# First layer's scores of a fused two-layer kernel: four fp32 products on 16 rows each, or two float32r products on 128 stacked rows

## The chip, the cores and the metric

One core of one Trainium2 chip runs the whole kernel. The metric is the device time of one execution in microseconds. The engines are TensorE (PE, with its weight loads PEld), VectorE (DVE), ScalarE (ACT), GpSimd (POOL) and SyncE (SP), which issues most of the DMAs.

## The reference

Two transformer-like layers over `x` of 16 x 256 x 256. What matters here is the attention of the first layer, with 16 heads of 16 values each:

```
q, k = rope(q), rope(k)                       # 16 heads, Dh = 16
scores = einsum('bhtd,bhsd->bhts', q, k) / sqrt(Dh)
scores = where(causal, scores, -inf)
probs = softmax(scores); out = einsum('bhts,bhsd->bhtd', probs, v)
return out @ w_out.T + b_out
```

Ahead of it stands a small cross attention with `fside`, behind it a category-dependent product and a gated feed-forward with blockwise fp4 rounding of activations and weights. The second layer (another attention, a routed feed-forward) follows. All inputs are float32.

## The kernel before

The program is written engine by engine; each engine runs its list in order, and semaphores tie the lists together. The first layer is a software pipeline over batches b from -2 to 17 (`B` is 16) with eight slots p each. A slot is one pair of heads: P = 8b + p. In a slot each engine does its part of the pair's attention, and beside it one piece of other work of the batch behind or ahead. All matmuls except those of heads and of some small products are written as three float32r products of a rounded part (`hi`) and a rest (`lo`): `matmuls3`.

The path of queries and keys, for batch b+1 during batch b:

- PE `project` (slots 1 and 2: queries, keys) writes even and odd components to bank 5; DVE `add_qk` adds the bias into `qk0`.
- POOL `rotate` (slot 3 in the steady state, both sides) multiplies with cosine and sine (two operations of 512 columns) and adds or subtracts (two of 256) into `QK0`. In the first batch DVE does the keys' part in `rotate_first`.
- SP `rotated` writes `QK0` to `d_rot` in device memory and reads it back with four DMAs into `Rs[b % 2]`, so that the 16 components of each head lie on 16 partitions that begin at a multiple of 32.

In slot p PE runs `scores(P + 1)`: for the two heads g, and for the two halves `st` of the queries, one fp32 product with 16 contracted rows, 128 queries and 128 or 256 keys (lines 338 to 342). Each appears as two instructions in the profile, eight in all. Then DVE `maxima` masks and takes the row maxima into `Ph`, ACT `exps` takes exponentials and sums, PE `turn_heads` transposes, ACT `copy_turned` copies to `PTh`, and PE `values` takes the product with the values every second slot.

The other work in a round of eight slots that the prediction names: slot 0 `turn_sums` (waits for both `multiply` of DVE into `hb`), `first_values`, `spread_sums`; slot 1 `project(b+1, 0)`, `turn_hidden`, on DVE `normal_out`, `hidden_steps` (L885, L888, L890) and `hidden_low`, on ACT `hidden_high` (`hqT_hi`); slot 2 `project(b+1, 1)`, `project_out`, DVE `add_attention`; slot 3 `turn_hidden`, `category`; slots 4 and 5 `down` and `project_v`, then `first_scores` and `turn_category`; slots 6 and 7 `gate` and `up`, with ACT `tanh` and DVE `gated`. POOL `rounded` does the rounding steps of the feed-forward (L1079, L1081, L1094), in slots 0, 2 and 4. During the first four batches the weights are rounded and split as well, in slots listed in `MEASURE`, `ROUND` and `TURN`. SP's list for a batch is `load_in(b+2)`, `load_category(b)`, `rotated(b+1)`. In the last rounds the generators of the second layer are started (`run(following, ...)`), and SP loads that layer's projection weights into `raw1`.

## Time and profile before

| what | value |
|---|---|
| median of 3 runs | 2471.0 us (2461.97, 2471.0, 2471.63) |
| span of the profiled execution | 2475.1 us |
| PE busy | 2335.6 us, 94% |
| DVE, ACT, POOL busy | 1840.2, 1276.7, 1039.9 us |
| first scores, last scores of the first layer | 49.6 us, 757.0 us |

The page gives the span of the profiled execution, from its first to its last instruction, and no separate time for it; it stands 4.1 us above the median of the three runs. Matmuls overlap in the records, so that the distance from one start to the next tells more than the duration of one. A line number with PE can be that of a helper: L55 is every product made with `matmuls`, L136 every transpose, L340 only the scores of the first layer.

### The profile page before, as it was taken

The page shows a single profiled execution, that of the slowest core. Times are in us where ns is not written, and L with a number is a line of the kernel's source. Part 1 is how long each engine was busy: PE and PEld are TensorE (multiplying, and loading weights), DVE is VectorE, ACT ScalarE, POOL GpSimd, SP SyncE. Part 2 cuts the span into 40 slices and gives each one's busy share as a digit, 9 for nine tenths or more (in the row PEclk, how much of TensorE's full clock was granted, in tenths as well). Part 3 has the DMA queues.
Part 4 walks back from the last instruction along what each step waited for, and adds up shares of the span by engine and source line. Part 5 has one row for each costly group of instructions (what it writes and reads, how often), then busy time and mean ns, then how long its engine had stood idle before and what let it go on. Part 6 is the DMA issues. An engine that isn't in the chain of part 4 may idle for free.

```text
span 2475.1 us, 55054 instructions
## 1 busy us (share of the span) xinstructions
PE 2335.6 (94%) x19136; PEld 2091.7 (85%) x19136; DVE 1840.2 (74%) x5136; ACT 1276.7 (52%) x3807; POOL 1039.9 (42%) x1090
## 2 busy tenths in 40 slices
PE   4899999999997799999999999889999999999999
PEld 3677887878876678888888887789999999999999
DVE  5777777777777766666666665568878888888876
ACT  2666566665654355555555555424325555555522
POOL 4545545446453545545545545123332222222063
PEclk7899999999998999999999999999999999999999
DMA  4321211211220221221122122132116777777444
GB/s 114 107 52 46 56 38 51 54 46 47 47 86 10 63 55 44 50 56 46 47 56 50 47 52 69 43 69 43 39 30 234 236 233 240 232 228 240 149 118 126
DMA packets 153080, 225.73 MB, mean 91 GB/s; under 512 B 54294, under 2 KB 123174, under 8 KB 142054
## 3 DMA queue, kind: packets, MB, share of 16 engines
q1 hardware_dynamic: 143942, 203.56, 28.6%
q0 software_dynamic: 8864, 18.66, 2.9%
q8 instruction: 154, 2.52, 0.5%
q14 instruction: 120, 0.98, 0.2%
HBM read 159.32 MB, written 27.16 MB: 75 GB/s over the span
## 4 chain that ended last, share of the span: by engine, by line
PE 69%; DVE 13%; POOL 7%; issue 5%; ACT 5%; DMA 1%; POOLq 0%; SPq 0%; DVEq 0%; ACTq 0%
PE bank L55 54%; PE bank L136 7%; PE bank L340 2%; POOL P L1743 2%; PE bank L367 2%; PE bank L1253 2%; PE bank L1293 1%; ACT Ph L622 1%; DVE xe L885 1%; ACT PTh L634 1%; POOL Qn L1768 1%; POOL Qn L1766 1%; DVE tb L1606 1%; POOL xr_lo L1775 1%; DVE Ph L771 1%
## 5 line engine op out<-in xcount | busy, mean ns | idle before, releaser
L1447 ACT ACTIVATE P<-P,mx 128x144 f32<-128x144 f32 x512 | 206.2, 405 | 264.1 <-DVE mx L1568 263.2
L2579 POOL DMA_INDIRECT xE<-d_y,ixs x78 | 112.5, 1442 | 336.0 <-PE bank L136 305.8
L55 PE MATMUL bank<-xD_hi,w1e_lo 128*128 128x256 f32 x880 | 251.1, 285 | 0.0
L55 PE MATMUL bank<-w2e_hi,hrD_hi 128*128 128x256 f32 x880 | 249.0, 283 | 0.0
L55 PE MATMUL bank<-w2e_lo,hrD_hi 128*128 128x256 f32 x880 | 248.9, 283 | 0.0
L55 PE MATMUL bank<-w2e_hi,hrD_lo 128*128 128x256 f32 x880 | 248.9, 283 | 0.0
L1743 POOL TENSOR_TENSOR P<-P,rs 128x512 f32<-128x512 f32 x128 | 133.3, 1042 | 273.8 <-DVE rs L1577 270.3
L1079 POOL TENSOR_TENSOR xe<-xe 128x704 f32<-128x704 f32 (+3 forms) x64 | 88.4, 1381 | 376.0 <-DVE xe L890 375.8
L55 PE MATMUL bank<-xD_lo,w1e_hi 128*128 128x256 f32 x880 | 245.9, 279 | 0.0
L55 PE MATMUL bank<-xD_hi,w1e_hi 128*128 128x256 f32 x880 | 245.6, 279 | 0.0
L2188 ACT ACTIVATE hD<-bank,b1E 128x256 f32<-128x256 f32 x312 | 127.0, 473 | 197.2 <-PE bank L55 182.8
L2281 DVE TENSOR_TENSOR hrD_lo<-hD,hrD_hi 128x512 fp32r<-128x512 f32 x284 | 197.3, 695 | 9.7
L622 ACT ACTIVATE Ph<-Ph,mx 128x128 f32<-128x128 f32 x256 | 101.0, 394 | 188.5 <-DVE mx L771 188.5
L2279 DVE CAST hrD_hi<-hD 128x512 fp32r<-128x512 f32 x284 | 121.4, 428 | 101.3 <-ACT hD L2188 100.7
L1568 DVE CUSTOM_DVE_ANT_0 P<-bank,maskb 128x144 f32<-128x144 f32 x512 | 126.1, 302 | 77.5 <-PE bank L1253 77.5
L771 DVE CUSTOM_DVE_ANT_0 Ph<-bank,maskb 128x128 f32<-128x128 f32 (+1 forms) x512 | 151.5, 350 | 28.1 <-PE bank L340 28.0
L55 PE MATMUL bank<-xr_hi,w_lo 128*128 128x256 f32 x512 | 157.7, 308 | 13.7 <-DVE fa L1640 11.0
L55 PEld LDWEIGHTS bank<-w2e_hi,hrD_lo 128*128 128x128 f32 x880 | 168.7, 192 | 0.0
L55 PEld LDWEIGHTS bank<-w2e_hi,hrD_hi 128*128 128x128 f32 x880 | 168.7, 192 | 0.0
L55 PEld LDWEIGHTS bank<-w2e_lo,hrD_hi 128*128 128x128 f32 x880 | 168.7, 192 | 0.0
L55 PEld LDWEIGHTS bank<-xD_hi,w1e_lo 128*128 128x128 f32 x880 | 165.6, 188 | 0.0
L55 PEld LDWEIGHTS bank<-xD_lo,w1e_hi 128*128 128x128 f32 x880 | 165.4, 188 | 0.0
(324 smaller groups left out, 8005.1 us busy)
## 6 DMA issues: line engine op xcount, KB each, us to landing
w1raw<-in_ew SPq DMA_DIRECT2D x39, 1024.0 KB, 5.7
w2raw<-in_ew SPq DMA_DIRECT2D x39, 1024.0 KB, 4.9
K<-Kn SPq DMA_DIRECT2D x256, 72.0 KB, 2.1
Q<-Qn SPq DMA_DIRECT2D x256, 64.0 KB, 2.0
d_ys<-oE SPq DMA_DIRECT2D x39, 256.0 KB, 2.7
d_rot<-QK SPq DMA_DIRECT2D x16, 512.0 KB, 2.9
Rs<-d_rot SPq DMA_DIRECT2D x64, 128.0 KB, 4.4
b2E<-in_eb SPq DMA_DIRECT2D x39, 128.0 KB, 3.6
```

What stands on the lines that cost most here:

```text
L55: inst = e.matmul(out, l, r, start=k == 0, stop=k == len(pairs) - 1)
L136: inst = e.transpose(o, i, ident[0:i.shape[0], 0:i.shape[0]])
L622: e.activation(dst[:, 0, :], dst[:, 0, :], ACT.Exp, bias=mx[:, 0, n:n + 1], scale=-1.0, accum_out=rs[:, 0, n:n + 1])
L771: inst = e.tensor_tensor_reduce(dst[:, st:2 * st + 1, :], bank[:, 128 * st:128 + 256 * st].rearrange("p (a n) -> p a n", n=128), mask(128 ...
L1079: e.tensor_tensor(x, x, s, ALU.add).then_inc(*po.up())
L1447: inst = e.activation(P1[t % 2][:, n, :], P1[t % 2][:, n, :], ACT.Exp, bias=mx1[t % 2][:, 2 * g + sg:2 * g + sg + 1], scale=-1.0, accum_ou ...
L1568: inst = e.tensor_tensor_reduce(P1[t % 2][:, 2 * sg + g, :], banks[6 + g][:, 144 * sg:144 * sg + 144], mask(144), -1.0, 1e30, ALU.add, ALU ...
L1743: e.tensor_tensor(P[:, :, 16:144], P[:, :, 16:144], r.broadcast_to((128, 4, 128)), ALU.mult).then_inc(*po.up())
L2188: inst = e.activation(hD[:, 2 * (n % 2) + m, :], halves(n)[:, m, :], ACT.Gelu if q < 0 else ACT.Gelu_apprx_tanh, bias=bias[:, f:f + 1])
L2279: e.tensor_copy(hr[0], h).then_inc(*vs.up())
L2281: e.tensor_tensor(hr[1], h, hr[0].bitcast(F32), ALU.subtract).then_inc(v_h, 1)
L2579: e.indirect_dma_start(out=xE[q % 2][c], out_offset=None, in_=d_y, in_offset=bass.IndirectOffsetOnAxis(ap=ixs[r % 4][:, c:c + 1].bitcast(U ...
```

## The change

- `QK0` becomes two tensors: `QKl` takes the rotated values, ACT (`heads_high`) writes their float32r rounding to `QKh`, POOL (`heads_low`) replaces `QKl` by the rest.
- DVE `add_qk` becomes `turn_qk`: bias addition and product with cosine and sine in one operation per component (512 columns each), into `rt0`. POOL's `rotate` keeps only the subtraction and the addition and moves to slots 1 and 2; `rotate_first` goes.
- SP writes for each side of q and k three copies to `d_rot`: for queries rounded, rounded, rest; for keys rest, rounded, rounded. `load_heads(L)` reads, for the two slots of pair L, 48 rows per head into partitions 0 to 47 and 64 to 111 of `QS`, which is cleared once at the start. The keys of the two heads have separate column blocks. There are two such buffers; they are used in turn.
- A slot's scores are two products on 128 rows: queries 128 to 255 with 2 x 256 keys into bank 0, queries 0 to 127 with 2 x 128 keys into bank 1. The maxima read them from there.
- SP's order: the loads for pair 4b+2, then `load_in`, the loads for 4b+3, `write_heads` for queries, `load_category`, `write_heads` for keys, the loads for 4b+4 and 4b+5. The second layer's weights are loaded after those for pair 63. In the stages behind it two semaphores are used again with an offset, with no change of order.

```diff
-        QK0, q0 = tile("QK0", 4, 256), tile("q0", 2, 256)
+        QKh, q0 = tile("QKh", 4, 256, dt=F32R), tile("q0", 2, 256)
...
-        rt0, qk0 = folded(rots[:, 0, :], (2, 2, 256)), folded(rots[:, 1, :], (2, 2, 256))
+        rt0 = [folded(rots[:, i, :], (2, 2, 256)) for i in range(2)]
...
+        QKl = tile("QKl", 4, 256, dt=F32R)
+        stack0 = tile("stack0", 12 * 256, dt=F32R)
+        QS = stack0.rearrange("p (h j x n) -> p h j x n", h=2, j=2, x=3)
...
-            def rotated(b, between=None):
-
-                e.wait_ge(g_rot, 2 * b + 2)
-                e.dma_start(d_rot[b].rearrange("q e p n -> p (q e) n"), QK0).then_inc(l_rw, 16)
-                if between is not None:
-                    load_block(between)
-                e.wait_ge(l_rw, 16 * (b + 1))
-                if b >= 2:
-                    e.wait_ge(p_S, 8 * (b - 1))
-                rows = d_rot[b].rearrange("q e (r j h) n -> j (e r) q (h n)", j=4, h=4)
-                for j in range(4):
-                    e.dma_start(Rs[b % 2][32 * j:32 * j + 16].rearrange("r q h n -> r q (h n)"), rows[j]
-                                ).then_inc(l_R[b % 2], 16)
+            def write_heads(b, qk):
+                if not 0 <= b < B:
+                    return
+                high, low = ((0, 1), 2) if qk == 0 else ((1, 2), 0)
+                src = [x[:, 2 * qk:2 * qk + 2, :].bitcast(F32) for x in (QKh, QKl)]
+                e.wait_ge(c_qh, 2 * b + qk + 1)
+                for s in high:
+                    e.dma_start(d_rot[b, qk, s].rearrange("e p n -> p e n"), src[0]).then_inc(l_rw, 16)
+                e.wait_ge(g_rot, 2 * b + qk + 1)
+                e.dma_start(d_rot[b, qk, low].rearrange("e p n -> p e n"), src[1]).then_inc(l_rw, 16)
+            def load_heads(L):
+                if not 0 <= L < 4 * B:
+                    return
+                b, h = divmod(L, 4)
+                if h == 0:
+                    e.wait_ge(l_rw, 96 * (b + 1))
+                if L >= 2:
+                    e.wait_ge(p_S, 2 * L - 2)
+                else:
+                    e.wait_ge(g_V, 4)
+                rows = d_rot[b].rearrange("x s e (r j g h) n -> g h (s e r) j x n", j=2, g=2, h=4)
+                for g in range(2):
+                    for x in range(2):
+                        e.dma_start(QS[64 * g:64 * g + 48, L % 2, :, x * (g + 1), :].bitcast(F32), rows[g, h][:, :, x, :]
+                                    ).then_inc(l_R[L % 2], 16)
 
...
-            rotated(0, 7)
+            write_heads(0, 0)
+            write_heads(0, 1)
+            load_block(7)
+            load_heads(0)
+            load_heads(1)
             load_block(8)
             load_category(0)
             for n in range(9, 12):
                 load_block(n)
+            load_heads(2)
             load_in(2)
-            for n in range(12, 15):
+            for n in range(12, 14):
                 load_block(n)
-            rotated(1)
+            load_heads(3)
+            load_block(14)
+            write_heads(1, 0)
+            write_heads(1, 1)
+            load_heads(4)
+            load_heads(5)
             load_block(15)
             load_x(2)
             for b in range(1, B):
+                if b == B - 1:
+                    run(following, 1)
+                load_heads(4 * b + 2)
                 if b + 2 < B:
                     load_in(b + 2)
+                load_heads(4 * b + 3)
+                write_heads(b + 1, 0)
                 if b == B - 1:
                     run(following, 1)
                 load_category(b)
-                if b + 1 < B:
-                    rotated(b + 1)
+                write_heads(b + 1, 1)
+                load_heads(4 * b + 4)
+                load_heads(4 * b + 5)
 
 
...
-                b, p = divmod(P, 8)
                 bank = banks[0:2]
                 if P:
                     e.wait_ge(v_mx, 2 * P)
-                if p == 0:
-                    e.wait_ge(l_R[b % 2], 64 * (b // 2 + 1))
-                j = [32 * (2 * (P % 2) + g) for g in range(2)]
-                q, k = ([Rs[b % 2][j[g]:j[g] + 16, x, p // 2, :] for g in range(2)] for x in range(2))
-                for st in range(2):
-                    for g in range(2):
-                        inst = e.matmul(bank[g][:, 128 * st:128 + 256 * st], q[g][:, 128 * st:128 * st + 128],
-                                        k[g][:, 0:128 * st + 128], start=True, stop=True)
-                inst.then_inc(p_S, 1)
+                L = P // 2
+                if P % 2 == 0:
+                    e.wait_ge(l_R[L % 2], 64 * (L // 2 + 1))
+                q, k = QS[:, L % 2, P % 2, 0, :], QS[:, L % 2, P % 2, 1:3, :]
+                e.matmul(bank[0][:, :], q[:, 128:256], k, start=True, stop=True)
+                e.matmul(bank[1][:, 0:256].rearrange("p (g n) -> p g n", g=2), q[:, 0:128], k[:, :, 0:128],
+                         start=True, stop=True).then_inc(p_S, 1)
 
...
+            def heads_high(b, qk):
+                if not 0 <= b < B:
+                    return
+                part = slice(2 * qk, 2 * qk + 2)
+                e.wait_ge(g_t, 2 * b + qk + 1)
+                e.activation(QKh[:, part, :], QKl[:, part, :].bitcast(F32), ACT.Copy).then_inc(c_qh, 1)
...
+                    if p == 1:
+                        heads_high(b + 1, 0)
+                    if p == 3:
+                        heads_high(b + 1, 1)
...
                         inst = e.tensor_tensor_reduce(
-                            dst[:, st:2 * st + 1, :], bank[:, 128 * st:128 + 256 * st].rearrange("p (a n) -> p a n", n=128),
+                            dst[:, st:2 * st + 1, :],
+                            banks[1 - st][:, 128 * (st + 1) * g:128 * (st + 1) * (g + 1)].rearrange("p (a n) -> p a n", n=128),
...
-            def add_qk(b, qk):
+            def turn_qk(b, qk):
                 if not 0 <= b < B:
                     return
                 e.wait_ge(p_qk, 2 * b + qk + 1)
                 if b:
-                    e.wait_ge(g_rot, max(2, 2 * b + qk - 1))
+                    e.wait_ge(g_t, 2 * b + qk - 1)
                 for eo in range(2):
-                    inst = e.tensor_scalar(qk0[:, qk, eo, :], halves(5)[:, eo, :], b_qk0[:, 2 * qk + eo:2 * qk + eo + 1],
-                                           None, ALU.add)
+                    inst = e.scalar_tensor_tensor(
+                        out=rt0[qk][:, eo], in0=halves(5)[:, eo:eo + 1, :].broadcast_to((128, 2, 256)),
+                        scalar=b_qk0[:, 2 * qk + eo:2 * qk + eo + 1], in1=rot0[:, eo:eo + 2, :], op0=ALU.add, op1=ALU.mult)
                 inst.then_inc(v_rq, 1)
-
-            def rotate_first():
-
-                rt = [OT0, Wc]
-                e.wait_ge(v_rq, 2)
-                for eo in range(2):
-                    e.tensor_tensor(rt[eo], qk0[:, 1, eo:eo + 1, :].broadcast_to((128, 2, 256)), rot0[:, eo:eo + 2, :],
-                                    ALU.mult).then_inc(*vs.up())
-                e.wait_ge(s_v, vs.n)
-                e.tensor_tensor(QK0[:, 2, :], rt[0][:, 0, :], rt[1][:, 0, :], ALU.subtract)
-                e.tensor_tensor(QK0[:, 3, :], rt[0][:, 1, :], rt[1][:, 1, :], ALU.add).then_inc(g_rot, 1)
 
...
             def rotate(b, qk):
                 if not 0 <= b < B:
                     return
                 e.wait_ge(v_rq, 2 * b + qk + 1)
-                for eo in range(2):
-                    e.tensor_tensor(rt0[:, eo], qk0[:, qk, eo:eo + 1, :].broadcast_to((128, 2, 256)), rot0[:, eo:eo + 2, :],
-                                    ALU.mult).then_inc(*po.up())
                 if b >= 1:
-                    e.wait_ge(l_rw, 16 * b)
-                e.wait_ge(s_p, po.n)
-                e.tensor_tensor(QK0[:, 2 * qk, :], rt0[:, 0, 0, :], rt0[:, 1, 0, :], ALU.subtract).then_inc(*po.up())
-                e.wait_ge(s_p, po.n)
-                e.tensor_tensor(QK0[:, 2 * qk + 1, :], rt0[:, 0, 1, :], rt0[:, 1, 1, :], ALU.add).then_inc(g_rot, 1)
-                e.wait_ge(g_rot, max(2, 2 * b + qk + 1))
+                    e.wait_ge(l_rw, 96 * b)
+                t = QKl[:, 2 * qk:2 * qk + 2, :].bitcast(F32)
+                e.tensor_tensor(t[:, 0, :], rt0[qk][:, 0, 0, :], rt0[qk][:, 1, 0, :], ALU.subtract)
+                e.tensor_tensor(t[:, 1, :], rt0[qk][:, 0, 1, :], rt0[qk][:, 1, 1, :], ALU.add).then_inc(g_t, 1)
+                e.wait_ge(g_t, 2 * b + qk + 1)
+            def heads_low(b, qk):
+                if not 0 <= b < B:
+                    return
+                part = slice(2 * qk, 2 * qk + 2)
+                e.wait_ge(c_qh, 2 * b + qk + 1)
+                e.tensor_tensor(QKl[:, part, :], QKl[:, part, :].bitcast(F32), QKh[:, part, :].bitcast(F32), ALU.subtract
+                                ).then_inc(g_rot, 1)
+                e.wait_ge(g_rot, 2 * b + qk + 1)
 
...
+            e.memset(stack0.bitcast(F32), 0.0).then_inc(g_V, 1)
+            e.wait_ge(g_V, 4)
...
-                    if b == 0 and p == 2:
-                        rotate(1, 1)
-                    if p == 3 and b != 0:
+                    if p == 1:
                         rotate(b + 1, 0)
+                    if p == 2:
+                        rotate(b + 1, 1)
+                        heads_low(b + 1, 0)
                     if p == 3 and b >= -1:
                         first_query(b + 2)
-                    if p == 3 and b >= 1:
-                        rotate(b + 1, 1)
+                    if p == 3:
+                        heads_low(b + 1, 1)
```

## Rows read from the trace of the kernel before

**Rows 1.** The page: span of the profiled execution.

```profile
span 2475.1 us, 55054 instructions
```

**Rows 2.** Busy time by stretch, 300 to 400 us, PE, PEld, DVE, ACT, POOL; PEclk, DMA share, GB/s.

```profile
300.00:400.00 100.00, 97.91 (x799) 80.80 (x798) 76.35 (x249) 60.11 (x217) 52.26 (x43) 1.00 0.22 53
```

**Rows 3.** Chain that ended last, 300 to 350 us: start us, us, what.

```profile
302.58 0.85 PE bank L340 x8
...
310.24 2.11 PE bank L55 x12
...
326.86 0.85 PE bank L340 x8
...
327.71 1.63 PE bank L55 x12
...
347.37 0.85 PE bank L340 x8
```

**Rows 4.** PE timeline, 404 to 450 us: start, us, instructions, [idle before <-releaser].

```profile
404.44 0.92 PE L340 MATMUL bank<-Rs 16*128 16x128 f32 x8
...
412.48 0.38 PE L136 MATMUL bank<-ident,rs 128*16 128x128 f32 x2 [0.21 <-DVE hb L919]
...
416.38 0.92 PE L340 MATMUL bank<-Rs 16*128 16x128 f32 x8
...
421.78 0.86 PE L367 MATMUL bank<-PTh,Vp 128*32 128x256 f32 x16 [0.69 <-ACT PTh L634]
...
426.58 0.92 PE L340 MATMUL bank<-Rs 16*128 16x128 f32 x8
...
428.15 0.82 PE L136 MATMUL bank<-ident,hq 128*128 128x128 f32 x6
...
431.70 0.86 PE L367 MATMUL bank<-PTh,Vp 128*32 128x256 f32 x16
...
442.90 0.92 PE L340 MATMUL bank<-Rs 16*128 16x128 f32 x8
...
444.54 0.43 PE L55 MATMUL bank<-wgT_hi,xqT_lo 128*128 128x352 f32 x1
```

**Rows 5.** ACT timeline of the same round.

```profile
414.63 0.60 ACT L660 ACTIVATE x_hi<-bank 128x512 fp32r<-128x512 f32 x1 [1.36 <-PE bank L55]
...
420.06 0.60 ACT L704 ACTIVATE hqT_hi<-bank 128x512 fp32r<-128x512 f32 x1
...
423.94 0.40 ACT L622 ACTIVATE Ph<-Ph,mx 128x128 f32<-128x128 f32 x1 [2.21 <-DVE mx L771]
```

**Rows 6.** DVE timeline of the same round.

```profile
405.41 0.29 DVE L771 CUSTOM_DVE_ANT_0 Ph<-bank,maskb 128x128 f32<-128x128 f32 x1 [0.27 <-PE bank L340]
...
418.97 0.88 DVE L829 TENSOR_SCALAR rot0s<-bank,b_qk 128x256 f32<-128x256 f32 x2 [0.41 <-PE bank L55]
...
420.36 0.88 DVE L885 SCALAR_TENSOR_TENSOR xe<-hb,qr 128x704 f32<-128x704 f32 x1
...
426.69 0.88 DVE L795 SCALAR_TENSOR_TENSOR X<-bank,b_out,X 128x256 f32<-128x256 f32 x2 [1.45 <-PE bank L55]
...
434.90 1.34 DVE L885 SCALAR_TENSOR_TENSOR xe<-c,qr 128x512 f32<-128x512 f32 x1
...
443.64 0.69 DVE L903 TENSOR_TENSOR xqT_lo<-bank,xqT_hi 128x512 fp32r<-128x512 f32 x1 [0.37 <-ACT xqT_hi L684]
```

**Rows 7.** POOL timeline: a startup row, then the same round.

```profile
2.25 1.96 POOL L1101 MEMSET Vp<- 128x1024 f32 x2
...
422.51 1.71 POOL L1079 TENSOR_TENSOR xe<-xe 128x704 f32<-128x704 f32 x1 [5.98 <-DVE xe L890]
...
427.51 2.50 POOL L1063 TENSOR_TENSOR rot0s<-rot0s,rot 128x512 f32<-128x512 f32 x2
```

**Rows 8.** Issues of the scores' operand loads: duration ns min/median/max, first and last start; landing.

```profile
L285 SPq DMA_DIRECT2D Rs<-d_rot x64: 319/423/916, 39.4 to 710.0; - x64
...
DMA to landing us min/median/max: 3.2/4.4/5.5
```

More of the change, by code:

```diff
@@ L169, in program @@
         P0 = tile("P0", 2, 256)
-        Rs = [tile(f"Rs{i}", 2, 4, 256) for i in range(2)]
+        QKl = tile("QKl", 4, 256, dt=F32R)
+        stack0 = tile("stack0", 12 * 256, dt=F32R)
+        QS = stack0.rearrange("p (h j x n) -> p h j x n", h=2, j=2, x=3)
         Vp = [tile(f"Vp{i}", 4, 8, 32) for i in range(2)]
@@ L766, in maxima @@
                     n = 2 * p + g
-                    bank, dst = banks[g], Ph[P % 2][g]
+                    dst = Ph[P % 2][g]
                     if P >= 2:
@@ L1008, in dve_ab @@
                     if p == 1:
-                        add_qk(b + 1, 0)
+                        turn_qk(b + 1, 0)
                         normal_out(b - 1)
@@ L1129, in pool_ab @@
                         rounded(n, *blocks[n][0].shape)
-                    if b == 0 and p == 1:
-                        rotate(1, 0)
                     if b >= B - 1:
@@ L1203, in sync_c @@
                 e.dma_start(zs[:, i, :], a[src].broadcast_to((128, B))).then_inc(l_c, 16)
+            yield
             for c in range(6):
@@ L1860, in program @@
             ("ew1", 2), ("ew2", 2), ("er", 2), ("ex", 2), ("eb", 2), ("o", 2), ("ix", 4), ("cg", 8)))
-        l_out = sem("l_out")
+        l_out, LOUT = l_in, 48 * B
         p_up, p_trD, p_trE, p_down, p_ty, p_rt, p_rank = (sem(f"p_{n}") for n in ("up", "trD", "trE", "down", "ty", "rt", "rank"))
-        c_g, c_f2, c_yr, c_w2E, c_gate = (sem(f"c_{n}") for n in ("g", "f2", "yr", "w2E", "gate"))
+        c_g, c_f2, c_w2E, c_gate = (sem(f"c_{n}") for n in ("g", "f2", "w2E", "gate"))
+        c_yr, CY = c_qh, 2 * B
         v_h, v_x, v_f2, v_R, v_yD, v_lg, v_mm, v_rk, v_slot, v_tab, v_cb, v_w2E = (sem(f"v_{n}") for n in (
@@ L2044, in sync_e @@
                 e.dma_start(out[j * 128:j * 128 + 128, :], R[:, j, :]).then_inc(l_out, 16)
-            e.wait_ge(l_out, 16 * 32)
+            e.wait_ge(l_out, LOUT + 16 * 32)
         def picked_up(e, i, n):
@@ L2133, in turn_y @@
                 if b:
-                    e.wait_ge(c_yr, b)
+                    e.wait_ge(c_yr, CY + b)
                 turn(e, [(halves(7)[:, st, k * 128:k * 128 + 128], y[:, k, st * 128:st * 128 + 128])
```

9 lines of the change are left out of this document (4 added, 5 removed).

## The prediction

> **What bounds the kernel now.** I took the stretches first. The change touches the first layer, and in its steady part PE is busy 97.91 of 100 us at granted clock 1.00, with DVE at 76, ACT at 60, POOL at 52 and the DMA engines at a share of 0.22 [rows 2]. That looks like a TensorE bound. The chain of waits comes second. It passes the scores (L340) four times between 302.58 and 347.37, each time for 0.85 us [rows 3]. These two starts are also one round apart: 44.8 us for one batch of eight slots, with eight scores slots. So half of the scores are on this chain; the others lie beside ACT and DVE work. The timelines come third. PE waits twice in a round: 0.21 us for DVE's `hb` before the sums are turned (412.48) and 0.69 us for ACT's `PTh` before the values (421.78) [rows 4]. These waits are short, but they are the places where a faster PE only waits longer. The question is therefore how many of the eight slots can shorten the round.
>
> **Price of a slot.** Before, a slot is eight instructions in 0.85 us [rows 3]. Afterwards it is two float32r matmuls, of 512 and of 256 moving columns. Twelve float32r matmuls of 256 columns take 1.63 us, twelve of 352 take 2.11 us [rows 3]. With some 0.2 us for entering the group that is 0.12 and 0.16 us each, near 0.4 ns a column. 512 columns come to 0.22 us (my extrapolation; the trace has no such matmul), 256 to 0.12, entering costs 0.1: 0.44 us. Against 0.85 a slot saves 0.41; where both neighbours are float32r already (slot 5, between the projection of v and the second half of `down`) another 0.15 goes, since two changes of type are gone: 0.6. If nothing but the two matmuls counted, a slot would save 0.5; if the wide one cost twice what I take, 0.2.
>
> **Where the saving can be used, over one round** [rows 4].
> - 404.44 to 412.48. Behind the scores go the maxima, four exponentials, tanh, the gate product and DVE's two `hb` products; PE stands waiting for these already. DVE waits only 0.27 us for these scores before its maxima at 405.41; until then it is in its products [rows 6]. So the maxima can begin at most 0.27 us earlier. The second slot of this stretch, beside that chain, gives nothing. Gain 0.27.
> - 412.48 to 421.78. ACT runs without a gap from `x_hi` at 414.63 to 419.95, then `hqT_hi` at 420.06 and `PTh` to 421.7 [rows 5]. Only the 0.11 us before 420.06 depend on PE. Two slots lie here; gain 0.11.
> - 426.58 to 431.70. DVE adds the attention (426.69 to 427.57) [rows 6] before it takes the maxima, so the scores at 426.58 are ready in time now; then exponentials, `hqT_hi` and `PTh` until the values at 431.70. Two slots, gain 0.
> - 431.70 to 442.9 is PE's own work. One slot, gain 0.6.
> - 442.90 to 444.54. A slot and the values stand before the gate, which needs `xqT_lo`, written by DVE from 443.64 for 0.69 us less its overlap (to about 444.3) [rows 6]. Of 0.41 us, 0.2 can be used. The rest of the round has no scores.
> Sum 1.2 us of a round of 44.8.
>
> **What is added.**
> - DVE: the two bias additions of 2x256 elements (0.88 us) become two fused products of 2x512. One such op lies between 0.44 (its 256 columns now) and 0.88 us (704 columns, L885); nearest is 0.69 for 512 columns from PSUM (L903) [rows 6]. Two make 1.35: +0.5 in slot 1 and +0.5 in slot 2. In slot 2 DVE has 1.45 us idle before `add_attention` (426.69). From the projection's end (418.97) both additions are in the way, 1.0 of the 1.45; the same DVE work can start about 0.35 earlier, because slot 1's scores are shorter. Room left: about 0.8 us.
> - POOL loses the two 2x512 products per side (2.50 us for two) and gains one difference of 512 columns per side; at half of that row, 1.25 us. Its differences of 256 columns stay, at about 0.7 by the same measure. Per round 5.0 less, 2.5 more: no load. But its place moves: `rotate(b+1,0)` now runs in slot 1, from about 420.4 to 422, beside DVE's `hidden_steps`, where POOL was idle (5.98 us before 422.51). What that does is visible elsewhere: L885 on 512 columns takes 1.34 us at 434.90 beside POOL's rotation and on 704 columns 0.88 at 420.36 with POOL idle [rows 6]. Three DVE steps stand there, so I take 0.6 us of delay, between 0 and 1.5. Up to 0.8 is free at `add_attention`; at 1.5 that add and all behind it come 0.7 later.
> - The same delay, with the 0.5 of the longer product, goes on to POOL's rounding of 704 columns: 422.51 to 427.5 [rows 7] becomes 428.6. PE turns that result at 428.15 [rows 4]: a wait of up to 0.5 us, and more if PE comes earlier. It is followed by 2.5 us of transposes and category, and by a slot that is 0.41 shorter, before the values at 431.70, which wait for ACT. I charge 0.2 us per round for these two, between 0 and 1.5.
> - ACT: two copies of 512 columns, 0.60 each [rows 5]. Each waits for POOL, and behind it are the next slot's exponentials. The first would run at about 422.2 to 422.8, and ACT waits 2.21 us for DVE's maxima there, until 423.94 [rows 5]; the second runs behind `PTh` of slot 3, where the next exponentials wait for DVE too. Nothing; if POOL is 1.5 late, the first ends at 424.3, but by then the maxima are late as well.
> - SP: 16 loads and 6 writes per round for 4 and 1. At 0.42 us an issue and 4.4 us to landing (5.5 at most) [rows 8], the four loads of a pair of slots take about 6 to 7 us. Each may start when the scores three slots earlier are done, 15 to 17 us ahead of their use (411.4 to 426.6). Across the batch border the way is longer: POOL's last difference to 433.6, a write to 437, loads to 443, needed at 449.2. Hidden; margin 6 us. Behind SP's wait for the first difference (to about 430.9) stands the category's load, which waits for PE's category product of slot 3 anyway. The weights of the next layer are loaded some 20 us later, in the last round, 25 us before their first use.
> - Start: POOL clears 3072 columns, 1.96 us for 2048 [rows 7], so 2.9 us in front of the first roundings, which PE, ACT and the first batch wait for; DVE loses its own rotation of about 3.3 us and gains 1.0. I set the two against each other, -1 to +3.
> Of SBUF the Trainium skill ("SBUF — State Buffer", section "SBUF: two separate sides") says that a VectorE operation with two SBUF inputs and a GpSimd operation that reads SBUF exclude each other for the whole instruction. The trace agrees with the 1.34 us above. By that rule each of the three steps could wait for one whole POOL operation of 0.7 us: nearer 1.5 than 0.6, and 0.7 us a round dearer.
>
> **Sum.** 1.2 - 0.2 = 1.0 us a round. Full rounds of this kind run from about 115 to 715 us: 13.4 of them, 13.4 us. The first two batches, where DVE measures weights, give perhaps 1 us together, the last one nothing, the start nothing. -14.4 us on a span of 2475.1 [rows 1], which is 4.1 us above the median of the runs, 2471.0; I take the difference off the median: 2456.6, say 2457.
>
> **Rivals.**
> 1. TensorE is the bound as the busy share says: 0.41 to 0.6 us in all 128 slots, 54 us, 2417. For it: 98% busy. Against it: the two waits, and ACT's unbroken run. 6%.
> 2. The four slots of the chain count in full: 4 x 0.45 x 15 = 27 us, 2444. For it: rows 3 as they stand. Against it: two of the four (404.44, 416.38) sit in front of DVE and ACT work that is nearly late itself. 21%.
> 3. The gain is eaten by the wait for POOL and DVE in slots 1 to 3, at 1.0 to 1.4 us a round: 2468 to 2475, or the wide matmul doesn't stream as extrapolated. 16%.
> 4. Slower: DVE's steps in slot 1 are each held by a POOL operation and the fused products cost 0.88, so `add_attention` is late by 2 us or more beyond its room, every round, and PE waits at the values. At 2.3 us late a round it passes the 1.2 gained by 1.1: +15 us, 2486. It decides from 1.2 us beyond the 0.8 of room. For it: 1.34 against 0.88. Against it: that delay needs POOL work of 2 us more than is there in slot 1. 11%.
> My forecast, 2449 to 2466 by its own terms, has 46%.
>
> **How the numbers follow.** Half a per cent, 12.4 us, is about what a measurement here tells from no change: faster means under 2458.6, slower over 2483.4. Faster: rivals 1 and 2 and just under three fifths of the forecast: 6 + 21 + 26 = 0.53. Slower: most of rival 4: 0.09. Same: the rest, 0.38. Range 2435 to 2476: it reaches to rivals 2 and 3 and leaves out 1, 4.
>
> **What would show it.** L340's place holds two matmuls of some 0.45 us a slot. PE's busy share falls from 98% to about 92%, and its waits before the values and before the turned sums grow from 0.2 and 0.7 to 1 us or more: that is the part of the saving that isn't used. The round goes from 44.8 to 43.8. DVE's steps in slot 1 (L885, L888, L890 on 704 columns) get longer, those on 512 columns shorter. If the round falls by more than 2 us, my reading of ACT's run and DVE's products as limits was wrong; if it grows, look at the wait before `add_attention` first, then for PE waiting on the operand loads.

## The result and the profile after

The changed kernel takes 2438.6 us (median, 2437.5 to 2440.4) against 2471.3 in the same session: ratio 0.987, interval 0.985 to 0.989. That is 32.7 us less; forecast were 14.3 less, at 2457. Sign and range held; the forecast gain is less than half of the measured one. The profiled execution spans 2438.6 us for 2475.1 [rows 1].

The stretch that answers to [rows 2]; the columns are busy time (instructions) of PE, PEld, DVE, ACT and POOL, then granted clock, DMA share and GB/s:

```profile
300.00:400.00 100.00, 91.56 (x713) 79.34 (x713) 79.35 (x265) 65.25 (x232) 41.80 (x33) 1.00 0.29 92
```

PE has gone from 97.9 to 91.6 us busy in 100. It was not the only limit before, and it is less of one now. (A round is the time from the first scores of one batch to those of the next.) The PE timeline of one round, 43.27 us long, against [rows 4]:

```profile
400.03 0.38 PE L136 MATMUL bank<-ident,rs 128*16 128x128 f32 x2 [0.72 <-DVE hb L955]
...
403.76 0.48 PE L372 MATMUL bank<-stack 128*128 128x512 f32 x1
404.07 0.28 PE L373 MATMUL bank<-stack 128*128 128x256 f32 x1
...
409.10 0.86 PE L399 MATMUL bank<-PTh,Vp 128*32 128x256 f32 x16 [1.66 <-ACT PTh L666]
...
415.79 0.88 PE L136 MATMUL bank<-ident,hq 128*128 128x128 f32 x6 [0.29 <-POOL hq L1135]
...
418.94 0.86 PE L399 MATMUL bank<-PTh,Vp 128*32 128x256 f32 x16 [0.20 <-ACT PTh L666]
...
424.03 0.40 PE L372 MATMUL bank<-stack 128*128 128x512 f32 x1
...
430.93 0.43 PE L55 MATMUL bank<-wgT_hi,xqT_lo 128*128 128x352 f32 x1 [0.27 <-DVE xqT_lo L939]
```

Look at the brackets: the two waits of [rows 4], 0.21 and 0.69 us, are 0.72 and 1.66 now, and there are new ones for POOL's `hq` and DVE's `xqT_lo`. All PE waits of a round were about 1 us and are 3.6. On DVE, against [rows 6], and on POOL, against [rows 7]:

```profile
407.74 1.38 DVE L921 SCALAR_TENSOR_TENSOR xe<-hb,qr 128x704 f32<-128x704 f32 x1
409.16 0.94 DVE L924 TENSOR_SCALAR xe<-xe 128x704 uint32<-128x704 uint32 x1
...
412.68 1.40 DVE L875 SCALAR_TENSOR_TENSOR rot0s<-bank,b_qk,rot 128x512 f32<-128x512 f32 x2
414.02 0.88 DVE L840 SCALAR_TENSOR_TENSOR X<-bank,b_out,X 128x256 f32<-128x256 f32 x2
...
422.45 0.69 DVE L921 SCALAR_TENSOR_TENSOR xe<-c,qr 128x512 f32<-128x512 f32 x1
```

```profile
13.49 2.66 POOL L1151 MEMSET stack<- 128x3072 f32 x1
...
407.65 0.72 POOL L1100 TENSOR_TENSOR QKl<-rot0s 128x256 f32<-128x256 f32 x1 [3.60 <-issue]
408.33 1.38 POOL L1101 TENSOR_TENSOR QKl<-rot0s 128x256 f32<-128x256 f32 x1
...
416.50 0.73 POOL L1101 TENSOR_TENSOR QKl<-rot0s 128x256 f32<-128x256 f32 x1
```

The multiplication of 704 columns grew from 0.88 to 1.38 us beside POOL's addition, which itself takes 1.38 instead of 0.73; the one of 512 columns, rid of POOL, fell from 1.34 to 0.69. `add_attention` follows the fused products with no idle time: the room of 0.8 us is used up, not overdrawn: it starts 1.94 us behind the products with `w_out`, where it was 1.93. The operand loads land in 2.7 us (median, 7.4 at most).

**Where the 36.5 us of the two profiles lie.** I take the starts of the same work in both; a minus is time saved.

- First scores 49.6 and 52.5 us: +2.9.
- The first two rounds, 41.65 and 44.41 us, became 40.38 and 39.75: -5.9.
- Twelve rounds of 44.79 became 43.27: -18.2. The last one and a half: -2.3. Last scores 756.4 and 732.9: -23.5 so far.
- Last product with `wo` of the second layer 1583.0 and 1558.3: -24.7, so the change of layers gave 1.2.
- Then, in code that both kernels share, 10.1 us within a stretch of 21.8, and 1.7 later.

The forecast has 1 us for the first two rounds together and nothing for the shared code. These two terms have views that show them.

The second batch, before and then after:

```profile
93.90:103.00 9.10, 7.49 (x39) 4.47 (x38) 2.82 (x17) 4.27 (x15) 2.22 (x3) 0.62 0.12 50
```

```profile
95.00:101.00 6.00, 3.96 (x34) 2.61 (x32) 3.02 (x19) 3.46 (x12) 2.46 (x3) 1.00 1.04 419
```

```profile
98.59 3.57 PE L55 MATMUL bank<-PT,fS 128*128 128x256 f32 x8
```

```profile
99.27 1.89 PE L55 MATMUL bank<-PT,fS 128*128 128x256 f32 x8
```

The first and third fence are before, the others after. The same eight products take 3.57 us at the low level (1.2 GHz) and 1.89 at 2.4. Before, the clock stood at 1.00 from 87 to 93 us with PE 88 to 100% busy; from 93 to 96 PE waited for `mx` and `PTh`, was busy 2.15 of 3 us, and the clock averaged 0.86; from 96 to 99 it was 0.50. After, it stayed at 1.00, although PE was no busier (3.96 of 6 us). Another dip, 0.80 from 121 to 129 us, is gone too.

In the second layer, before (waits from 1637 to 1646 us: engine, line, releaser, us, times, longest; two rows of the timeline), then the stretch before and after:

```profile
PEld bank L55 <- issue: 6.4, 2, 6.0
PE bank L55 <- issue: 6.3, 2, 5.8
DVE xD_lo L2259 <- remote: 5.8, 1, 5.8
```

```profile
1640.62 0.97 POOL L2569 DMA_INDIRECT d_ix<-tid,sli  x1 [0.30 <-issue]
...
1644.53 0.56 PE L55 MATMUL bank<-hrD_hi,f2a_hi 128*128 128x256 f32 x1 [5.78 <-issue]
```

```profile
1638.00:1648.00 10.00, 3.14 (x15) 2.54 (x14) 2.55 (x8) 0.84 (x2) 2.90 (x3) 0.67 0.38 43
```

```profile
1610.00:1620.00 10.00, 10.00 (x88) 10.00 (x87) 8.33 (x28) 2.00 (x6) 4.72 (x4) 1.00 0.26 55
```

PE stands for 5.8 us on a product that waits for nothing that the profile shows, DVE and ACT stand too, POOL from 1641.6, and the clock is low behind it. I call this the stop. I find it by the time of the products 400 to 500 after the last `wo` product ("the 100 products"): 21.8 us here, 11.7 in the changed kernel. It is the open question of the second half of the experiments.

### The profile page after: what moved, and what is told of

It reads as the page before. It is cut to its first block, busy times and chain, and to the rows that moved or that the text cites. A ratio compares the mean times of both kernels' runs of the same rounds, so it can differ in the third digit from the quotient of the medians.

```text
span 2438.6 us, 53844 instructions
## 1 busy us (share of the span) xinstructions
PE 2262.9 (93%) x18368; PEld 2057.9 (84%) x18368; DVE 1840.2 (75%) x5132; ACT 1291.7 (53%) x3839; POOL 1005.2 (41%) x1063
## 4 chain that ended last, share of the span: by engine, by line
PE 61%; DVE 15%; ACT 8%; POOL 7%; issue 6%; DMA 1%; POOLq 0%; SPq 0%; DVEq 0%; ACTq 0%
PE bank L55 51%; PE bank L136 6%; ACT Ph L654 2%; POOL P L1786 2%; ACT Ph L656 2%; PE bank L1296 1%; DVE Ph L815 1%; ACT PTh L666 1%; PE bank L1336 1%; DVE xe L921 1%; DVE sgs L945 1%; PE bank L399 1%; POOL Qn L1811 1%; POOL Qn L1809 1%; DVE hb L955 1%
## 5 line engine op out<-in xcount | busy, mean ns | idle before, releaser
L55 PEld LDWEIGHTS bank<-xD_hi,w1e_hi 128*128 128x128 f32 x880 | 165.0, 187 | 0.0
```

The lines of the kernel that those rows point to most:

```text
L55: inst = e.matmul(out, l, r, start=k == 0, stop=k == len(pairs) - 1)
```

## The experiments

Most kernels were timed against the kernel before on the same chip; there were four chips (A for the first four, B for the next four, C, D). Times of before: A 2471.3, B 2482.4, C 2472.5, D 2482.4 us. Because chips differ by 11 us, I compare ratios, and read rounds (whose medians repeat to 0.02 us on all chips) from profiles. The changed kernel itself was not timed on B.

**The changed kernel again.**

> The changed kernel once more, unaltered. Two theories of the 32.7 us. A: some 23 us come from the first layer (3 before the second batch is done, 1.4 us in each of 15 rounds), and 9 to 10 us are a stop of all engines at 1638.8 us of the profiled run before, in a later stage that the change leaves alone. Then runs of before fall in two groups, near 2462 and near 2471, and this kernel stays at 2437 to 2441, or shows 2448 if the stop can hit it too. B: all 32.7 us belong to the change; then before stays at 2471 and this at 2439, each within 2 us.

2439.35 us, ratio 0.987 [0.985, 0.988], and nine executions of before between 2469.6 and 2472.4: by the signs written down that is theory B. The profiles below decide otherwise: the stop lies in shared code, and every profile of the kernel before has it. One of the first four executions of before took 2461.97 us, 9 less than the others; it was not profiled, so whether it escaped the stop is not known.

**Products alone.** The kernel before with

```diff
-        Rs = [tile(f"Rs{i}", 2, 4, 256) for i in range(2)]
+        Rs = [tile(f"Rs{i}", 2, 4, 256, dt=F32R) for i in range(2)]
```

> The kernel before with one thing changed: queries and keys are read as float32r, so that each score product is one instruction on its 16 rows; the rests are left out of the scores. All of DVE, ACT, POOL and SP is as before. A (TensorE time of the slots is what counts, limited elsewhere): a slot falls from 0.85 to about 0.4 us, the round from 44.8 to 43.6, a little less than in the change since POOL's rounding is still late in slots 4 and 5: 14 to 18 us faster than before. B (the gain is mostly the lighter and moved work of POOL and DVE): at most 5 us faster.

It leaves the rests out of the scores. 2455.3 us, ratio 0.994 [0.992, 0.995]: -16 us. Round 43.52 in most batches, so products alone give 1.27 us of the 1.52. In the stretch with slot 5 this kernel's four products on 16 rows take 0.26 us more than the two stacked ones (8.52 and 8.26 us in the second table below); that is what is missing. Three rounds took 45.1, and in each the clock was at the low level for 3.4 us, here from 415.9:

```profile
415.00:420.00 5.00, 5.00 (x35) 4.63 (x28) 2.87 (x13) 2.85 (x10) 4.78 (x3) 0.66 0.00 0
```

Its second batch had the low clock as well (45.72 us) and it still had the stop.

**Products doubled.** In the changed kernel:

```diff
+                e.matmul(bank[1][:, 0:256].rearrange("p (g n) -> p g n", g=2), q[:, 0:128], k[:, :, 0:128],
+                         start=True, stop=True)
+                e.matmul(bank[0][:, :], q[:, 128:256], k, start=True, stop=True)
```

> The changed kernel, with each of the two products of a slot issued twice. A slot goes back to some 0.75 to 0.85 us of TensorE, the rest of the change stays. A: most of the 1.4 us a round is lost, 15 to 20 us slower than the changed kernel, 2455 to 2459. B (POOL and DVE relief is the gain): at most 5 us slower, 2444.

2447.6 us, ratio 0.991 [0.989, 0.992]: +8.3, between the two theories (15 to 20, at most 5). Round 43.98, +0.71. A second pair adds 0.44 us to a slot (277.57 to 278.01 below), eight of them 3.5, so a fifth of what is added shows. PE timeline:

```profile
277.57 0.48 PE L372 MATMUL bank<-stack 128*128 128x512 f32 x1
277.89 0.28 PE L373 MATMUL bank<-stack 128*128 128x256 f32 x1
278.01 0.40 PE L375 MATMUL bank<-stack 128*128 128x512 f32 x1
```

**Clearing first.** POOL clears the stack before `first_query(0)`, whose wait for a load (6.86 us) it then fills:

```diff
-            first_query(0)
             for x in wdT:
...
             e.memset(stack0.bitcast(F32), 0.0).then_inc(g_V, 1)
             e.wait_ge(g_V, 4)
+            first_query(0)
```

> The changed kernel, with POOL's clearing of the stacked operands (2.67 us at 13.49) moved ahead of the first query addition, where POOL stands idle for the first loads. A: the first scores come 2.8 us earlier (52.4 to 49.6) and 1 to 3 us of it reach the end: 2436 to 2438. Rival: the weights' loads and DVE set the pace of the first 100 us, nothing reaches the end: 2438.6.

2438.7 us, ratio 0.987 [0.986, 0.989]. The first scores come at 49.7 instead of 52.5 us, as before the change, and in its profile the third batch starts at 128.7 us where the four profiles of the changed kernel have 131.3 to 132.8. The time is within 1 us of the changed kernel's, though: at the end it is not separated from nothing.

**The data path alone.** The changed kernel with fp32 products, eight instructions on 48 rows, banks as before:

```diff
+                q, k = ([QS[64 * g:64 * g + 48, L % 2, P % 2, x * (g + 1), :].bitcast(F32) for g in range(2)]
+                        for x in range(2))
+                for st in range(2):
+                    for g in range(2):
+                        inst = e.matmul(bank[g][:, 128 * st:128 + 256 * st], q[g][:, 128 * st:128 * st + 128],
+                                        k[g][:, 0:128 * st + 128], start=True, stop=True)
```

> The changed kernel with its whole new data path (turn_qk, rotate in slots 1 and 2, the rounded parts and rests, six writes and the stacked loads, the order of SP), but a slot's scores as before: for each head and half of the queries one fp32 product, now on the 48 stacked rows of its head, two banks as before. So TensorE has the old 0.85 us per slot and the other engines have the new work. Theory A (my terms: TensorE's scores carry the gain, the data path costs little and frees little): the round stays within 0.3 us of the old 44.79, and the total is 2471 minus what does not lie in the rounds (the low clock of the second batch, 4.7 us, and the stop of 10 us near 1640, if they belong to the data path or to the placement of the tensors): 2455 to 2471. Theory B (the data path carries much of it: the maximum part of 0.25 us per round that the 16-row float32r run left over): round 44.5, 3 to 4 us less again. Theory C (the new work costs and the products pay for it): round above 44.8, total 2475 or more. The run of the products alone had a round of 43.52 against 43.27 of the changed kernel, so I expect 44.5 and 2458, with the second batch at the full clock.

2484.2 us, ratio 1.0005 [0.9996, 1.0014]. Round 45.16: 0.37 longer than before, so theory C; I had expected 44.5. This experiment and "Products alone" separate the two sides, in two orders: the new work costs 0.37 us a round under slow products, and the fast products then give 45.16 - 43.27 = 1.89; or the fast products come first and give 1.27, and the new work costs nothing more. The two do not add: the fast products hide what the new work costs. The cost sits in pair 4 of the table below (0.57, of which 0.22 come back in pair 5), where PE turns `hq` in slot 3. PE timeline of this kernel, at the place of 428.15 in [rows 4], where there was no wait:

```profile
292.24 0.89 PE L136 MATMUL bank<-ident,Ph 128*128 128x128 f32 x6
293.42 0.88 PE L136 MATMUL bank<-ident,hq 128*128 128x128 f32 x6 [0.28 <-POOL hq L1137]
```

Medians over nine steady rounds, read from the starts in the traces, us from the scores of pair p (modulo 8) to the next:

```
pair            0     1     2     3     4     5     6     7    round
before        6.12  5.82  3.79  6.41  4.04  6.26  6.02  6.31  44.79
products      5.76  5.82  3.37  6.62  3.61  6.60  5.60  6.16  43.53
data path     6.12  5.82  3.80  6.41  4.61  6.04  6.03  6.34  45.16
after         5.69  5.82  3.09  6.78  4.15  6.27  5.25  6.25  43.28
doubled       5.88  5.82  3.44  6.43  4.48  6.07  5.59  6.25  43.96
heads late    5.68  5.82  3.09  6.77  3.53  6.88  5.25  6.25  43.26
proj. first   5.68  5.82  3.09  6.29  4.62  5.98  5.25  6.25  42.97
all three     5.69  5.81  3.09  5.65  4.62  5.98  5.31  6.25  42.40
```

Read columns 2 and 3: faster scores shorten the first by 0.70 and the next is 0.37 longer. What ends it is ACT's `PTh`, at the end of the run that begins with `x_hi` and not with these maxima: the values start 7.15 us behind `x_hi` before and 6.92 after, but 4.43 and 4.71 us behind the maxima. Column 1 never moves.

The starts of scores are not the places at which the prediction counts. The same medians from one of its places [rows 4] to the next, by their times in the kernel before; two of them are in no row there:

```profile
440.64 1.89 PE L55 MATMUL bank<-fT,q 128*128 128x256 f32 x8
...
449.21 0.92 PE L340 MATMUL bank<-Rs 16*128 16x128 f32 x8
```

```
from     to       before  products  data path  after   after less before
404.44   412.48     8.05      7.68       8.04   7.77   -0.28
412.48   421.78     9.30      9.08       9.31   9.08   -0.22
421.78   431.70     9.92      9.83      10.26   9.83   -0.09
431.70   440.64     8.94      8.52       8.95   8.26   -0.68
440.64   444.54     3.90      3.75       3.90   3.74   -0.16
444.54   449.21     4.68      4.69       4.70   4.59   -0.09
round              44.79     43.55      45.16  43.27   -1.52
```

The cost of the new work is in one stretch, 421.78 to 431.70: 0.34 more with slow products, nothing with fast ones.

**The heads' work in slot 3.** `rotate`, `heads_high`, `heads_low` of both sides there:

```diff
-                    if p == 1:
+                    if p == 3:
                         rotate(b + 1, 0)
-                    if p == 2:
                         rotate(b + 1, 1)
```

> The changed kernel with the rotation of both sides, the rounding and the rests all in slot 3, as before the change had its rotation, so that nothing of it runs beside DVE's steps of slot 1. If the slowed DVE steps of slots 1 and 2 (the multiplication of 704 columns took 1.38 us against 0.88 in before) cost something on the chain: round 43.27 falls by 0.3 to 0.4 us, total 2434. If they are covered: round unchanged, total within 1.5 us of 2439. If the later writes to device memory make the first scores of a batch wait: round longer, total above 2445.

2461.1 us, ratio 0.992 [0.991, 0.993]. DVE's multiplication is back at 0.88 us, pair 4 is 0.62 shorter, pair 5 0.61 longer, where PE waits about 1.09 us for `PTh`; the round stays at 43.26. The slowed DVE steps are shown to be POOL's doing, and to be covered. The total is not within the 1.5 us that I had written for this case: the first two rounds grew to 42.63 and 41.42, 4 us together, and this profile has the stop (the 100 products in 19.9 us).

```profile
410.33 0.88 DVE L920 SCALAR_TENSOR_TENSOR xe<-hb,qr 128x704 f32<-128x704 f32 x1
```

**The keys' projection ahead of the values.**

```diff
-                    if p % 2 == 0:
+                    if p % 2 == 0 and p != 2:
                         values(P // 2 - 1)
...
                         project(b + 1, 1)
+                        values(P // 2 - 1)
```

> The changed kernel with the keys' projection ahead of the values' product in slot 2, where PE stands 1.66 us each round for ACT's copy of the transposed weights. If that wait is one of TensorE's own that only an order can fill: round shorter by 0.8 to 1.6 us, total 2415 to 2427. If the round is bound by a chain that runs through DVE and ACT (theory that the slots are chains and TensorE has slack): the wait reappears at the next slot and the round stays within 0.3 us, total 2436 to 2440. I expect half: 43.27 to 42.6, total 2429.

2454.0 us, ratio 0.989 [0.988, 0.991]. Round 42.97, 0.30 less: the edge of the second theory, and half of the 0.67 that I expected. 0.49 us is gained in pair 3 and half a microsecond goes back in pair 4, the wait for POOL's chain, as in the table.

**All three.**

> The early clearing of the stack, the heads' work in slot 3 and the keys' projection ahead of the values' product together. If the three are independent their gains add: 2439 minus 1, minus what the run with the work in slot 3 gains and minus what the run with the projection first gains, about 2424. If they fill the same idle time of TensorE: no less than the better of the two alone.

2443.6 us, ratio 0.985 [0.983, 0.986]. Round 42.41: 0.87 less, where the parts gave 0.02 and 0.30. That is more than their sum: by columns 3 and 5 each frees what limited the other (1.12 in pair 3, where the projection alone gave 0.49, and no 0.61 lost in pair 5).

**Controls, and the stop**, on a third chip.

> The kernel before, unaltered, to see its profile beside the others of this chip. Question 1, the stop of all engines near 1640 us (products 400 to 500 after the last wo product take 21.7 us in the shown profile of before, 11.7 in four profiles of kernels with the stacked scores on one chip, but 19.1 to 23.5 in four such kernels on another chip). If it belongs to the kernel before: 19 to 24 us here, and 11.7 in the changed kernel. If it belongs to the chip or to where the tensors lie in its memory: the same in both on one chip. Question 2, the low clock in the second batch: here again about 8 us at 1.2 GHz, second round 44.4.

> The changed kernel, unaltered, on the same chip as the one before. If the stop is the chip's and both kernels have it here, the gain is that of the rounds and the start, 24 us, ratio 0.990; if it is the kernel's, 33 us again, ratio 0.987.

> The kernel before with d_rot as long in device memory as the change makes it (half again), nothing else changed: the tensors behind it, the table d_ix among them, lie 8 MB further on. If the stop comes from where they lie: the products 400 to 500 take 11.7 us as in the changed kernel, total 8 to 10 us under the kernel before. If it does not: same as before within 2 us, and the cause stays open.

Before, unaltered: 2470.6 us, the stop there, the 100 products in 18.1 us. After, unaltered: 2438.6, ratio 0.986 [0.984, 0.988], no stop, 11.7. Up to the last `wo` product the two differ by 24.0 us. Longer tensor: 2470.3, ratio 0.999 [0.998, 1.000], stop as before. Where the tensors lie is not it.

> The three edits together (round 42.41), with the heads' work left in slots 1 and 2 for the first batches, where moving it made the first two rounds 3.9 us longer. If the start then is that of the changed kernel with the early clearing: rounds 39.2, 39.7 and 42.4, total 14 us under the changed kernel on this chip. If the low clock of the first rounds decides the start and comes at random: between 9 and 14 under it.

2428.1 us, ratio 0.981 [0.980, 0.983], the fastest kernel here: 10.5 under the changed one on the same chip, between the two bounds. First rounds 39.16 and 40.47 (3.4 us at the low level from 119.5), steady 42.40.

```diff
-                    if p == 1:
+                    if p == (3 if b >= 1 else 1):
                         heads_high(b + 1, 0)
```

(and the same condition for POOL's two rotations and first rest). PE is 94.6% busy in it, DVE 82:

```profile
300.00:400.00 100.00, 94.63 (x719) 80.83 (x718) 82.28 (x271) 67.08 (x240) 44.45 (x35) 1.00 0.31 97
```

**Four more for the stop**, on a fourth chip.

> The kernel before with the same bytes to and from d_rot in as many DMAs as the changed kernel has (6 writes and 16 loads a batch instead of 1 and 4), nothing else. If the stop goes by where the queue of SP stands, it moves or is gone: products 400 to 500 in 11.7 us, or the stop at another product, total 6 to 10 us less. If it does not, the stop stays at the products 438 to 441 and the total within 3 us of before; the round stays 44.79 in both, since the loads have 30 us of room.

2533.5 us, ratio 1.020 [1.018, 1.022]; stop at products 432 to 435. My "30 us of room" was wrong: with all writes behind POOL's last difference and 16 loads behind them, PE waits 30.6 us in 15 batches for `Rs<-d_rot`, and the round is 47.4 to 50.2 us. That wait is 2.0 us of the 2.6 to 5.4 by which rounds grow; the rest goes with the clock, which in nearly every round is at the low level for 3.4 or 6.8 us, as from 425 us. I take it that the changed kernel's transfers are hidden because it sends each side and each pair on its own; no run tests that alone.

```profile
L290 SPq DMA_DIRECT2D Rs<-d_rot x256: 303/423/1847, 40.2 to 762.1; - x128
...
  PE bank L345: 30.6, 15
```

```profile
425.00:432.00 7.00, 6.36 (x26) 5.67 (x27) 3.49 (x13) 2.89 (x11) 0.00 (x0) 0.52 0.00 0
```

> The kernel before with one of the two semaphores that the change uses again (that of the last writes of the output), nothing else; the numbers of the semaphores behind it move by one. If the stop belongs to them: gone, total 6 to 10 us less. If not, which I expect: as before.

2481.0 us, ratio 0.999 [0.998, 1.000]; stop at 441. As expected.

> The kernel before, unaltered: products 400 to 500 after the last wo product in 18 to 22 us, stop at the products 438 to 441, on whatever chip this is.

> The changed kernel, unaltered. On the chips seen so far with it: 11.7 us for those 100 products. If this is the chip on which four kernels with its data path had a stop: 19 to 23 us, at the products 415 to 425, and then the stop belongs to the chip as well as to the program.

One execution each: 2481.1 and 2456.7 us, both with the stop, the 100 products in 22.31 and 22.34 us. In the stretches (before, then after) PE works 2.9 and 2.5 us of 10:

```profile
1637.00:1647.00 10.00, 2.93 (x16) 2.32 (x15) 1.58 (x7) 0.84 (x2) 2.90 (x3) 0.74 0.39 53
```

```profile
1610.00:1620.00 10.00, 2.53 (x14) 2.03 (x14) 2.49 (x12) 0.55 (x2) 4.58 (x4) 0.71 0.26 52
```

So on this chip both have it, at different products (445 to 448 and 418 to 421), and the spans differ by 24.0 us, 2479.0 to 2455.0. The four kernels with the new data path on chip B had it too, at the products 415 to 425. The chips differ elsewhere as well: the products 6400 to 7000 take 71.1 us in every profile of A and C and 76.5 to 79.2 in every one of B and D, whichever the kernel. That and the longer stop make the 11 us between the chips.

## Why the prediction was wrong, by its steps

**What bounds the kernel: right.** Two other engines limit most slots; the full TensorE bound (2417) did not come. PE's busy share fell to 92%, as said.

**Price of a slot: a little low.** Between fp32 groups the pair takes 0.53 us to the next start instead of 0.85 (the pair and the change of type; 0.35 between float32r neighbours), and it starts 0.17 us closer to the group in front of it. Together that is 0.50 less, and 0.70 less between float32r neighbours, where I had 0.41 and 0.6. The 512-column product is 0.23 to 0.42 us to the next start, the extrapolation was 0.22.

**Where the saving is used: right in its places, low in size.** By the second table, measured for foretold: up to the turned sums 0.28 for 0.27; up to the values 0.22 for 0.11; PE's own work 0.68 for 0.6; up to the gate 0.16 for 0.2; the rest of the round 0.09 for 0. ACT's run held as I read it, but I took its slack from the end of one record to the start of the next, and ACT's records overlap when they follow each other without a wait. Before, `hqT_hi` starts at 420.06, 0.31 us behind the instruction in front of it; after, 0.09 behind. So 0.22 us were free and not 0.11:

```profile
419.75 0.20 ACT L624 ACTIVATION_READ_ACCUMULATOR Ph<-Ph,mx 128x1 f32 x1
420.06 0.60 ACT L704 ACTIVATE hqT_hi<-bank 128x512 fp32r<-128x512 f32 x1
```

```profile
407.30 0.20 ACT L656 ACTIVATION_READ_ACCUMULATOR Ph<-Ph,mx 128x1 f32 x1
407.39 0.59 ACT L736 ACTIVATE hqT_hi<-bank 128x512 fp32r<-128x512 f32 x1
```

**The charge for DVE and POOL: the step of the round that failed.** For 421.78 to 431.70 I took a gain of 0 and a charge of 0.2 us a round. The stretch became 0.09 shorter: 0.29 of the 0.5 us that the round is off. The delay is there, 0.34 us by the data path alone, where PE waits for `hq` and then has nothing but its own work up to the values. I named what pays for it, the shorter slot in front of the values, and charged the 0.2 all the same.

**What is added: right in its rows.** Fused products 1.40 for two (1.35 foretold), clearing 2.66 (2.9), ACT's roundings 0.63 (0.60), the DVE steps 0.9 longer (0.6, between 0 and 1.5), the wait for POOL's `hq` 0.29 (up to 0.5). By my use of the Trainium skill ("SBUF — State Buffer", section "SBUF: two separate sides") each of the three steps could wait for one whole POOL operation, 0.7 us more a round; two were held, by 0.50 and 0.41 us. This trace agrees with the direction, for both engines (POOL's addition took 1.38 instead of 0.73). A whole operation per step was too much because each step came when POOL's was under way: the multiplication, at 407.74, 0.63 us before the end of the addition that started at 407.65, and the step at 409.16 0.55 us before the end of the next.

**The sum.** Net per round 1.52 instead of 1.0, and 12 full rounds plus 2.3 us for the last one and a half instead of 13.4: 20.5 us where I had 13.4. That is 7 us of the 22 between -14.4 and the -36.5 of the profiles. The start with the first two rounds is 2 more (3.0 instead of 1), and 13 lie behind the first layer, which the sum puts at nothing without a reason: 1.2, 10.1 and 1.7. That is the largest step that failed. *The first two batches*: 5.9 us instead of 1, of which 4.7 in the second. I valued DVE's and POOL's steps there and did not look at the granted clock; two stretches at 1.2 GHz stood in the trace of before. The second round was 44.0 to 44.4 us in the kernel before (43.0 with the longer tensor), 45.7 with products alone, 42.2 with the data path alone, whose clock was 0.79 from 95 to 103 us and 1.00 from 121 to 129, and 39.7 in all four profiles of the changed kernel. Both halves together are not enough either: three of the reordered kernels have a low stretch there again (41.42, 41.57 and 40.47 us). What in the start keeps the clock up is open. Against it stand 2.9 us for the start, where I had 0; -1 to +3 was the bound. On chips C and D the start and the first two rounds together gave 1.6 and 1.5 us, so this term is small there. *The stop*: 10.1 us in the shown pair, in code that the change does not touch. On chip D, where both kernels have it, the gain is 24 to 26 us, ratio 0.990; on A and C, where only kernels with before's data path do, it is 32 to 34.

So of the 32.7 us, some 24 come from the first layer, the start and the change of layers, as the two profiles of chip D show over the whole program and those of chip C up to the last `wo` product; the rest comes with the absence of the stop. What stops all engines is not settled: not the place of the tensors, not the one semaphore tried, and more transfers moved it by some products and did not remove it. That the changed kernel escapes it on two chips is a fact of these runs, not an explained gain; on D it has it, and on B its variants do.

**The rivals.** Four chain slots in full (27 us, 2444) is nearest in time, right in the places and not in the sizes. Its four are the chain's scores at 302.58, 308.60, 314.91 and 326.86 ([rows 3] and the two rows here).

```profile
308.60 0.85 PE bank L340 x8
...
314.91 0.88 PE bank L340 x8
```

They answer to 436.88, 442.90, 404.44 and 416.38 in the round of [rows 4], and the stretches in which they lie are where the round did shrink, by 0.68, 0.16, 0.28 and 0.22 us instead of four times 0.45. Its 27 us stand against the 24 without the stop, of which 20.5 come from the rounds that it prices; that it is near is in part luck. The round rules out the first (2417) and the third (no gain). The fourth, slower, needed 2 us of delay beyond the room of 0.8; 0.9 came, within that room.

## What to carry to other kernels

When an engine is 98% busy beside others with short waits, price a saving from one wait to the next, take the slack from starts and not from recorded ends, and set a delay and the saving that lies behind it in the same stretch against each other before charging the delay. In this kernel 1.89 of the 4.5 us by which the fast products made PE less busy shortened the round (97.67% of 45.16 us against 91.56% of 43.27), and one reordering that alone gave nothing and one that gave 0.3 gave 0.87 together. Read the granted clock of every stretch, not only of the steady part: three rounds of "Products alone" lost 1.6 us each to it. And compare starts of shared code before crediting a change with the whole difference.

## What the runs showed of the hardware

fp32 products on 48 rows take what those on 16 rows take. Groups of the same 90 us, the kernel before and the data path alone (columns: count, busy us, mean ns):

```profile
L340 PE MATMUL bank<-Rs 16*128 16x256 f32 x64 | 9.6, 376 | 0.0
```

```profile
L375 PE MATMUL bank<-stack 48*128 48x256 f32 x64 | 9.6, 377 | 0.0
```

The stop: PE, DVE and ACT stand from within POOL's four indirect transfers of small rows (1636.07 to 1641.59 us before); the changed kernel has the same four at 1611.26 to 1616.89 and no stop. With the low clock behind it the 100 products take 6.4 to 12.6 us more, at a nearly fixed product per kernel and chip. In it, the 96 packets of the software queue took 4.3% of sixteen engines' 10 us before (1640 to 1650), 0.7% for 96 in the changed kernel's stretch without one (1615 to 1625):

```profile
q0 software_dynamic: 96, 0.00, 4.3%
```

```profile
q0 software_dynamic: 96, 0.00, 0.7%
```

Whether the packets are held up or hold up the rest, no run here tells.
